# A selective scan cut into halves: second halves in one wide scan, the carry added to their first columns by GpSimd

## The reference

```python
# selective scan: DI = 256 channels, DS = 16 states, L = 256 positions, b = 4 batches
u = silu(causal_conv4(in_proj_w @ context) + conv_b)
dt_lo, Bm, Cm = split(x_proj_w @ u)
delta = softplus(dt_proj_w @ dt_lo + dt_proj_b)
A = -exp(A_log)
for t in range(L):
    state = state * exp(delta_t[..., None] * A) + (delta_t * u_t)[..., None] * B_t[:, None, :]
    y_t = (state * C_t).sum(states)
x = x + tanh(g_xattn) * ((y + D * u) * silu(layernorm(x)))
# experts: two shared blocks and 8 experts of width 176, the best 2 of 8 per token
hn = layernorm(x)
h = silu(hn @ wg.T) * (hn @ wu.T)          # 10 blocks of 176 for every token
x = x + tanh(g_ffn) * (shared_out + sum of the two chosen experts, weighted)
```

## Time and profile before

| what | us |
|---|---|
| median of 3 runs | 270.29 (270.20 to 270.37) |
| the profiled execution, its own time | 269.66 |
| its span, first to last instruction | 267.7 |
| busy: TensorE, VectorE, ScalarE, GpSimd | 222.0, 227.0, 175.5, 182.0 |
| mean granted clock of TensorE | 0.923 |

### The profile page before, as it was taken

The page is one execution under the profiler, slowest core; times in us unless marked ns, Lnnn a source line. Parts: engine busy times, 40 slices in busy tenths (PEclk is TensorE's granted clock), DMA queues, the critical chain, the costliest instruction groups (busy, mean ns, idle before and its releaser), DMA issues.

```text
span 267.7 us, 4168 instructions
## 1 busy us (share of the span) xinstructions
PE 222.0 (83%) x1093; PEld 167.9 (63%) x1093; DVE 227.0 (85%) x590; ACT 175.5 (66%) x536; POOL 182.0 (68%) x187
## 2 busy tenths in 40 slices
PE   8841983576847589999968979999999989999994
PEld 3421652354625368778746767687787778678883
DVE  1789999999999999999999998999798999563231
ACT  3579989965799695857577886584674562251121
POOL 0238999999899999998574998989586574120000
PEclk9985698559997599999999997999999999999999
DMA  6789953000025000000071000000000000000000
GB/s 175 230 269 386 364 189 157 0 0 2 0 80 240 0 1 0 22 1 0 24 271 44 1 20 2 2 0 22 0 1 21 2 0 0 20 2 1 21 0 20
DMA packets 9559, 17.34 MB, mean 65 GB/s; under 512 B 824, under 2 KB 8800, under 8 KB 8928
## 3 DMA queue, kind: packets, MB, share of 16 engines
q1 hardware_dynamic: 9248, 16.94, 18.3%
q10 hardware_dynamic: 288, 0.16, 0.2%
HBM read 15.97 MB, written 1.11 MB: 64 GB/s over the span
## 4 chain that ended last, share of the span: by engine, by line
PE 40%; DVE 24%; POOL 22%; issue 7%; DMA 3%; ACT 2%; SPq 1%; DVEq 0%; POOLq 0%; ACTq 0%
PE psD L451 14%; PE psU L599 11%; POOL dbu L1010 11%; DVE hs L902 7%; POOL acc L1034 5%; POOL wlo L1054 3%; PE psM L583 3%; DVE ag L984 3%; DVE prod L913 3%; PE psU L609 3%; DMA x_sb<-in_x 3%; PE psU L610 3%; PE psU L611 3%; DVE hs L896 3%; DVE hcat L811 2%
## 5 line engine op out<-in xcount | busy, mean ns | idle before, releaser
L1010 POOL TENSOR_TENSOR dbu<-du,bb 128x512 f32<-128x512 f32 x64 | 80.5, 1273 | 9.9 <-DVE du L379 4.6
L642 ACT ACTIVATE psA<-delta,aneg 128x127 f32<-128x127 f32 (+1 forms) x256 | 78.2, 357 | 6.2 <-DVE hs L902 3.4
L1034 POOL TENSOR_TENSOR acc<-acc,prod 128x512 f32<-128x512 f32 x42 | 54.2, 1291 | 16.4 <-DVE prod L913 15.0
L599 PE MATMUL psU<-wup,hnT 128*128 128x352 f32 x160 | 58.9, 493 | 1.7 <-DVE hcat L807 1.0
L771 ACT ACTIVATE tg<-psU 128x176 f32<-128x176 f32 x80 | 24.7, 315 | 48.3 <-PE psU L599 29.4
L902 DVE TENSOR_TENSOR_SCAN hs<-psA,ends,dbu 128x128 f32<-128x128 f32 x128 | 50.4, 456 | 0.2 <-DVE prod L913 0.2
L451 PE MATMUL psD<-wdn,hT 128*128 128x256 f32 x224 | 50.2, 380 | 0.0
L451 PEld LDWEIGHTS psD<-wdn,hT 128*128 128x128 f32 x224 | 42.1, 190 | 5.8 <-DVE wtok L977 0.3
L913 DVE TENSOR_TENSOR prod<-hs,psC 128x512 f32<-128x512 f32 x64 | 41.9, 673 | 0.6 <-DVE hs L896 0.4
L984 DVE SCALAR_TENSOR_TENSOR ag<-tg,psU 128x176 f32<-128x176 f32 x80 | 25.3, 327 | 17.8 <-ACT tg L771 17.5
L896 DVE TENSOR_TENSOR_SCAN hs<-psA,dbu 128x512 f32<-128x512 f32 x32 | 38.3, 1209 | 0.3 <-POOL dbu L1010 0.3
(11 more groups left out here) (117 smaller groups left out, 317.3 us busy)
## 6 DMA issues: line engine op xcount, KB each, us to landing
bb<-brows SPq DMA_DIRECT2D x3, 2048.0 KB, 7.1
hcat<-in_w_up SPq DMA_DIRECT2D x2, 880.0 KB, 8.9
wup<-in_w_up SPq DMA_DIRECT2D x2, 880.0 KB, 11.6
wdn<-in_w_down SPq DMA_DIRECT2D x1, 1664.0 KB, 14.1
x_sb<-in_x SPq DMA_DIRECT2D x4, 256.0 KB, 6.8
bb<-brows SPq DMA_DIRECT2D x1, 1024.0 KB, 4.7
out<-outb SPq DMA_DIRECT2D x8, 128.0 KB, 1.7
sel<-in_sel SPq DMA_DIRECT2D x1, 768.0 KB, 6.0
```

The lines of the kernel that those rows point to most:

```text
L599: last = pe.matmul(dst, hnT[:, b % 2, k, lh * P:(lh + 1) * P], wup[:, j // 2, k, :], start=(k == 0), stop=(k == KT - 1))
L642: last = act.activation(dst[:, j, h, c:], delta[:, b % 2, h, l0 + c:l1], ACT.Exp, scale=aneg[:, h * DS + s0 + j:h * DS + s0 + j + 1])
L1010: pool.tensor_tensor(tile(dbu[:, m % DBU_RING]), du[:, b % 2, :, l0:l1].unsqueeze(1).broadcast_to(shape), bb[:, b % 2, s0:s0 + NS, l0:l1]. ...
L1034: pool.tensor_tensor(acc[:, p % 2], before, prod[:, i % PROD_RING], ALU.add).then_inc(s_add, 1)
```

## The change

1. A second half is one scan of 512 columns as well (L902 and its loop go). Its starting states come in through the data: `decay` on ScalarE computes, once a batch, exp(A x delta) at position 128 for all states (`dec`, two activations of 128x16); `carry` on GpSimd, two for each batch, multiplies `ends` by it (128x16); and `fix` on GpSimd, one for each second half, adds the carry to the first column of each row of `dbu` (128x4). The scan waits for its `fix`. The first columns of `psA` stay zero for all steps, so the six copies of zeros go and all activations are 127 columns wide.
2. `spread_c` does two steps at a time: four products into one bank of `psC`, 32 tasks instead of 64. Task i waits for the products of steps up to 2i - 3.
3. `sel` is 96x32 instead of 96x32x128; the weights of a product are one column of it, read with stride 0 over 128 columns.
4. The transposition of a group of `hcat` is a task of its own (`turn`), `down` is one group, and `hidden` is numbered by groups; so TensorE's and ScalarE's lists place them one by one, for all tiles.
5. All orders are written anew. On VectorE `delta2:0` now stands ahead of `tap0:1`, and the taps of batch 3 stand ahead of scan:31, where they stood behind scan:35. On ScalarE `z_norm:0` stands between `soft_exp:0` and `soft_log:0`, `skip:0` ahead of `xproj_out:0`. On GpSimd `z_stats:3` stands in the beginning.
6. A switch `HALVED` for each batch (all True) would let a batch be scanned in one piece; with all True it does nothing.

```diff
     "GpSimd": """
-        z_stats:0 z_stats:1 z_stats:2 first:0 scan:0 scan:1 scan:2 scan:3 scan:4 weights_lo:0 weights_lo:1
-        scan:5 scan:6 scan:7 scan:8 weights_lo:2 scan:9 weights_lo:3 weights_lo:4 scan:10 scan:11 scan:12 prod:9
-        variance:0 delta0:1 prod:10 scan:13 scan:14 prod:11 delta1:1 features_lo:0 delta2:1 prod:12 scan:15
...
+        z_stats:0 z_stats:1 z_stats:2 z_stats:3 first:0 scan:0 scan:1 scan:2 scan:3 scan:4 weights_lo:0
+        weights_lo:1 scan:5 weights_lo:2 scan:6 scan:7 scan:8 carry:0 scan:9 fix:8 fix:9 carry:1 weights_lo:3
+        weights_lo:4 fix:10 scan:10 prod:9 fix:11 scan:11 scan:12 scan:13 fix:12 fix:13 fix:14 variance:0
+        prod:10 delta0:1 scan:14 prod:11 delta1:1 fix:15 prod:12 features_lo:0 delta2:1 prod:13 scan:15 scan:16
...
-        sel = sb("sel", [P, 2 * DS, P], BF16)
+        sel = sb("sel", [P, 2 * DS], BF16)
...
+        def row(n):
+
+            return sel[0:XROWS, n:n + 1].broadcast_to([XROWS, P])
...
                 elif task == "spread_c":
-                    b, s0, l0, l1 = step_range(i)
...
                     if i >= 2:
-                        pe.wait_ge(s_prod, i - 1)
-                    for j in range(NS):
-                        last = pe.matmul(psC[:, i % 2, j * P:(j + 1) * P], sel[0:XROWS, DS + s0 + j, :],
-                                         parts[:, b % 2, l0:l1], start=True, stop=True)
+                        pe.wait_ge(s_prod, 2 * i - 2)
+                    for m in (2 * i, 2 * i + 1):
+                        b, s0, ns, l0, l1 = step_range(m)
+                        for j in range(ns):
+                            c = m % 2 * L + j * (l1 - l0)
+                            last = pe.matmul(psC[:, i % 2, c:c + l1 - l0], row(DS + s0 + j),
+                                             parts[:, b % 2, l0:l1], start=True, stop=True)
                     last.then_inc(s_cps, 1)
...
+                elif task == "turn":
+                    t, q = divmod(i, NG)
+                    take_misc(s_ht, i + 1)
+                    pe.wait_ge(s_mul, group_end(i) + 1)
...
                 elif task == "down":
-                    for g in range(NG * i, NG * (i + 1)):
-                        down(g)
+                    down(i)
...
-                if m % DS in (0, 1) and m >= DS:
-                    act.copy(dst[:, :, :, 0], tile(zeros[:, 0:NS * EH])[:, :, :, 0])
-                c = 1 if l0 == 0 else 0
-                for j in range(NS):
+                for j in range(ns):
                     for h in range(EH):
-                        last = act.activation(dst[:, j, h, c:], delta[:, b % 2, h, l0 + c:l1], ACT.Exp,
+                        last = act.activation(dst[:, j, h, 1:], delta[:, b % 2, h, l0 + 1:l1], ACT.Exp,
...
+                elif task == "decay":
+                    act.wait_ge(s_delta, i + 1)
...
+                    for h in range(EH):
+                        last = act.activation(dec[:, i % 2, :, h], aneg[:, h * DS:(h + 1) * DS], ACT.Exp,
+                                              scale=delta[:, i % 2, h, P:P + 1])
+                    last.then_inc(s_dec, 1)
...
-                    if l0 == 0:
-                        dve.tensor_tensor_scan(hs[:, i % 2], psA[:, i % DA_RING], dbu[:, i % DBU_RING], 0.0,
-                                               ALU.mult, ALU.add).then_inc(s_scan, 1)
-                    else:
-                        dve.wait_ge(s_ends, ends_of(i))
-                        for c in range(NS * EH):
-                            row = slice(c * P, (c + 1) * P)
-                            last = dve.tensor_tensor_scan(hs[:, i % 2, row], psA[:, i % DA_RING, row],
-                                                          dbu[:, i % DBU_RING, row], ends[:, i % HALF, c:c + 1],
-                                                          ALU.mult, ALU.add)
-                        last.then_inc(s_scan, 1)
+                    if second_half(i):
+                        dve.wait_ge(s_fix, ends_of(i))
+                    dve.tensor_tensor_scan(hs[:, i % 2], psA[:, i % DA_RING], dbu[:, i % DBU_RING], 0.0,
+                                           ALU.mult, ALU.add).then_inc(s_scan, 1)
...
+                elif task == "carry":
+                    b, j = divmod(i, 2)
+                    k0, k1 = j * HALF // 2, (j + 1) * HALF // 2
+                    pool.wait_ge(s_ends, HALF * b + k1)
+                    pool.wait_ge(s_dec, b + 1)
+                    if b >= 1:
+                        pool.wait_ge(s_fix, HALF * b)
+                    pool.tensor_tensor(carry[:, k0:k1].rearrange("p k c -> p (k c)"),
+                                       ends[:, k0:k1].rearrange("p k c -> p (k c)"),
+                                       dec[:, b % 2, NS * k0:NS * k1].rearrange("p s h -> p (s h)"),
+                                       ALU.mult).then_inc(s_carry, 1)
+                elif task == "fix":
+                    heads = dbu[:, i % DBU_RING].rearrange("p (c l) -> p c l", l=P)[:, :, 0]
+                    pool.wait_ge(s_dbu, i + 1)
+                    pool.wait_ge(s_carry, 2 * (i // DS) + (1 if i % HALF < HALF // 2 else 2))
+                    pool.tensor_tensor(heads, heads, carry[:, i % HALF], ALU.add).then_inc(s_fix, 1)
...
-        "sel": np.broadcast_to((rows[:, None] == np.arange(2 * DS))[:, :, None],
-                               (XROWS, 2 * DS, P)).astype(ml_dtypes.bfloat16),
+        "sel": (rows[:, None] == np.arange(2 * DS)).astype(ml_dtypes.bfloat16),
```

More of the change, by code:

```diff
@@ L63, in group_last_unit, with first_half, second_half, sum_of @@
     return (min(GROUPS[g][1] * P, FCAT) - 1) // FF
+HALVED = (True, True, True, True)
 def part_end(p):
-    return (p + 1) * HALF
+    b, h = divmod(p, LH)
+    return DS * b + HALF * (h + 1) if HALVED[b] else DS * (b + 1)
 def step_range(m):
     b, n = divmod(m, DS)
+    if not HALVED[b]:
+        return b, n, 1, 0, L
     half, k = divmod(n, HALF)
[L75 to L85, removed]
+    return b, NS * k, NS, half * P, (half + 1) * P
+def first_half(m):
+    return HALVED[m // DS] and m % DS < HALF
+def second_half(m):
+    return HALVED[m // DS] and m % DS >= HALF
+def sum_of(m):
+    b, n = divmod(m, DS)
+    earlier = sum(2 if HALVED[c] else 1 for c in range(b))
+    if not HALVED[b]:
+        return earlier, n, DS
+    return earlier + n // HALF, n % HALF, HALF
+def tiles_in(total):
+    return next(m // DS * LH + (LH if not HALVED[m // DS] else m % DS // HALF + 1)
+                for m in range(STEPS) if sum_of(m)[0] == total)
+def group_end(g):
+    return NU * (g // NG) + group_last_unit(g % NG)
 ORDER = {
     "SyncE": """
-        xproj:0 dt:0 xproj:1 dt:1 xproj:2 dt:2 finish:0 finish:1 xproj:3 dt:3 finish:2 finish:3 finish:4
+        xproj:0 dt:0 xproj:1 dt:1 xproj:2 dt:2 finish:0 xproj:3 finish:1 dt:3 finish:2 finish:3 finish:4
         finish:5 finish:6 finish:7
@@ L109 @@
[L109 to L112, removed]
+        project:0 xproj:0 dt:0 spread_b:0 spread_b:1 project:1 spread_c:0 spread_c:1 prod:0 prod:1 prod:2 prod:3
+        spread_c:2 xproj:1 prod:4 spread_c:3 spread_c:4 prod:5 dt:1 prod:6 prod:7 y_sum:0 spread_c:5 spread_c:6
@@ L113 @@
+        down:25 up:73 up:74 down:26 up:75 up:76 turn:28 up:77 down:27 up:78 up:79 turn:29 down:28 turn:30
+        down:29 turn:31 down:30 down:31
     """,
     "ScalarE": """
[L115 to L117 removed]
@@ L138 @@
[L138 to L142, removed]
+        load:0 project_out:0 tanh_u:0 skip:0 xproj_out:0 dt_out:0 soft_exp:0 z_norm:0 soft_log:0 spread_b:0
@@ L459, in spread_b @@
                 for i in range(4):
-                    last = pe.matmul(psU[:, k, i * P:(i + 1) * P], sel[0:XROWS, 4 * k + i, :], parts[:, 0, 0:P],
+                    last = pe.matmul(psU[:, k, i * P:(i + 1) * P], row(4 * k + i), parts[:, 0, 0:P],
                                      start=True, stop=True)
```

345 lines of the change are left out of this document (177 added, 168 removed).

## The result

The new kernel takes **259.70 us** (median of 4 runs, 259.23 to 261.67), the old one in the same session 270.25 (269.10 to 270.37, 4 runs): a ratio of 0.963, with a 95% interval of 0.9575 to 0.969. The forecast was 265.8 with a range of 261.0 to 269.7. The profiled execution took 259.31 us, with a span of 257.5.

A forecast was written before the change was run, and what follows sets the result against it. GpSimd and VectorE were taken to bound 22 to 118 us, VectorE and TensorE 118 to 226, TensorE the rest. 0.5 - 4.0 - 1.0 = -4.5 us from 269.66 gave 265.2, plus 0.63 for the median: 265.8, range 261.0 to 269.7.

The forecast's parts named there:

- Narrow scans, 12.1 us off VectorE: On VectorE, replacing the second halves' narrow scans with wide ones takes off 12.1 us, 6.05 of it in batches 0 and 1.
- `fix` and `carry` at 0.26, 10.4 us: On GpSimd, 40 new small operations at 0.26 us each add 10.4 us, 5.2 of it in batches 0 and 1.
- ScalarE nothing: On ScalarE, `decay` at 0.19 us less the copies of zeros adds 0.4 us, hidden in idle time; taken as nothing.
- Stride-0 loads nothing: On TensorE, one-hot weights read with stride 0 cost 0; 5.8 us if slow. Rival of slow loads: 271.6 us, chance 0.04.
- The start, 1.1 us earlier: At the start, the smaller `sel` lets x land earlier, so GpSimd's first product comes 1.1 us earlier; bounds 0.3 and 1.5.
- First stage, +1.1 on GpSimd: From 22 to 118 us, GpSimd has 5.2 more to do, 3.0 idle and starts 1.1 earlier: ends 1.1 us later.
- VectorE alone would gain 7.15, but GpSimd has no room: From 22 to 118 us, VectorE's possible gain of 6.05 + 1.1 = 7.15 us is held back by GpSimd's extra work.
- I take half of 8.1, 4.0: From 118 to 226 us, at most 8.1 us of TensorE's idle and low-clock time can come out; half, 4.0, was taken.
- all of it passes: Rival: the second stage's whole 8.1 and the tail's 1.0 come out, 9.1 us off, 261.2 us; chance 0.13.
- TensorE's work does not shrink: From 118 to 226 us, TensorE's work stays the same, so only 6.4 us idle and some 1.7 of low clock can go.
- Tail, 1.0: After 226 us, `down` placed group by group among the units takes out 1.0 us of TensorE's idle time.
- slower by `fix`: Rival: scans wait for `fix` in GpSimd's queue, at 0.66 us per small operation: 4.1 us slower, 274.4 us; chance 0.11.

The follow-up runs named there:

- run 8: New kernel with the full 768 KB `sel` read with stride 1: 260.74 us; also the old kernel with `spread_c` in pairs: 273.33 us.
- run 5: New kernel without `carry` and `fix`, so its output lacks what the first halves hand on: 259.80 us.
- run 6: New kernel with one, then four more 128x4 additions on GpSimd ahead of each `fix`: 263.12 us and 275.64 us.
- run 1: New kernel with second halves scanned as before, four narrow scans each, without `decay`, `carry` and `fix`: 269.23 us.
- run 3: Old kernel and old lists with wide second-half scans, `decay`, `carry` and `fix` added: 276.43 us.
- experiment 4: Old kernel and old lists with wide scans but without `carry` and `fix`, second halves starting from zero; run twice: 272.52 us and 271.92 us.
- run 7: New kernel with the four `down` groups of a tile in one block at the place of the last: 283.65 us.

## Why the prediction was right and wrong

- **Narrow scans, 12.1 us off VectorE: right.** The scans' rows went from 88.7 to 76.7, 12.0 us; the engine's whole busy time by 11.6.
- **`fix` and `carry` at 0.26, 10.4 us: right.** 0.25 and 0.22, 9.5 us by the groups; 0.20 for a `fix` that nothing holds up.
- **ScalarE nothing: right.** A `decay` takes 0.30 us, not 0.19; scans wait 1.1 us in all for `psA`.
- **Stride-0 loads nothing: right.** 104 ns. By the rule of the Trainium skill ("TensorE: Matmul & The Clock Gate", weight-path perf modes) the term was 0. The trace agrees: 104 ns with stride 0, 107 to 109 with full blocks, and nothing near the 190 to 197 of 4-byte data.
- **The start, 1.1 us earlier: right, as run 8 bears out** (1.0 between medians of two sessions). In the rows of the new kernel, `split0` starts at 14.35 and GpSimd's first product at 20.49, forecast 13.75 and 20.07, since this execution was already 0.7 us late when the taps of the convolution were done; that of run 5 was not, and has them at 13.73 and 19.86.

```profile
14.35 0.40 DVE L904 TENSOR_TENSOR psM<-psM,parts 64x256 f32<-64x256 f32 x1
```

```profile
20.49 7.41 POOL L1045 TENSOR_TENSOR dbu<-du,bb 128x512 f32<-128x512 f32 x6 [2.04 <-DVE du L416]
```

- **First stage, +1.1 on GpSimd: near in size, half right in its reason.** Step 31's sum on GpSimd ended at 114.50 and ends at 114.74, 0.2 later, and scan:32 ends 0.8 later. GpSimd is level with the limit (run 6), but so are the others (run 5). "VectorE alone would gain 7.15, but GpSimd has no room" took the old lists' balance over. The new lists put more of VectorE's work ahead of scan:32 (with narrow scans it ends 7.0 later), and the wide scans of this stage pay for that: without them the kernel is 4.3 us slower.
- **Second stage, "I take half of 8.1, 4.0": the step that failed.** Of the 8.1 nearly all came out: TensorE's idle time fell from 6.4 to 1.1 us (5.3) and the low clock went (1.7), 7.0 for 4.0. With the tail (1.0) and the loss ahead (0.5) it made -4.5 from 118 us on; measured were -10.2, a little over the "all of it passes" rival's 9.1: 7.0 here, 1.4 in the tail, and 1.8 that the sum had at nothing by "TensorE's work does not shrink". Its products didn't get fewer, but its busy time fell by more than the clock's part. One source is `spread_c` in pairs, 1.9 us by the groups behind 118 us (7.2 for 60 products, then 5.3 for 56); how much of that passes into the union with other products no view tells. The reason given, that engines which hand units to and fro never both fill, is refuted: TensorE fills 106.88 of 108 us, and from 154 to 166 us TensorE has 11.86, VectorE 11.52 and GpSimd 11.71 of 12. The lists take 3.8 us of its idle time out with narrow scans still in place, and the wide scans 2.9 more (6.7 to 3.8). That the lists place `down` and `turn` one by one is what the prediction had priced in the tail alone; run 1's batch 2, 9.0 us shorter, says that the lists' part was there.
- **Tail, 1.0: right, a little small.** TensorE's idle time behind 226 us was 4.15 (the 4.45 of the prediction counts 0.3 us behind the end of the span) and is 2.7, 1.4 less; what is left lies at and behind the last addition, which starts at 254.83 us of 257.5, as before.

- **The rival "slower by `fix`"** was no phantom: it is what happens when the wide scans are put into the old lists (run 3). The price was near 0.2, not 0.66, and it still cost some 9 us there; that the old lists leave GpSimd no place for it is the reading of runs 3 and 4.

So the gain belongs to no part alone. The lists alone give 1.4 us, the wide scans alone lose 6, together they give 10.5. I had priced the lists as a placement of the parts; by these runs they are the part that turns VectorE's saving into TensorE's busy time, in batch 2 above all. Open is which of the moves in the lists does it: they were not taken apart one by one, as the orders of the engines depend on each other (only `down`, run 7, and the pairs were).

## What to carry to other kernels

When a change comes with all orders written anew, price the orders as a part of their own: take the idle time of the engine with the fixed work as what can come out, and don't halve it by habit. A saving on one engine shows only if the lists move the next engine's work into it, and wide scans in lists made for narrow ones can be slower than before. Taking work away and adding some of the same kind answer different questions: here, in the first stage, removal gave 0 and addition cost about one for one, and only both together say that the engines are level.

## What the runs showed of the hardware that was not expected

- An operation of VectorE and those of GpSimd held each other up. `sz` (128x512, both inputs in SBUF) took 0.65 to 0.70 us in 39 of the 56 times that the fourteen profiled executions have it. In the other 17 it took 1.00 to 6.02, and each time it ended 0.55 us after an operation of GpSimd had ended. When GpSimd had four in a row, `sz` outlasted all four (5.84 and 6.02 us, experiment 4). The other way round, operations of GpSimd beside `sz` were longer: a `fix` 0.65 to 0.93 us for 0.20, a product (L1016 in experiment 3) 1.73 for 1.27. The rows show the pattern; no experiment moved `sz` to test it.
- GpSimd's additions of 128x4 cost 0.21 us each, back to back and without a wait, in a sequence of four.
